# A graph layer with a mixer and experts: two bias rows added as one-row matmuls in PSUM instead of VectorE additions

## The reference, cut to what matters

```python
h = xn                                        # graph network, three layers
for l in range(3):                            # relu, relu, sigmoid
    agg = segment_sum(h[src], edge_type * N_NODES + dst)       # one sum for each relation and node
    h = act(einsum('rnd,rde->ne', agg.reshape(8, N_NODES, -1), W[l]) + h @ root[l] + bias[l])
...                                           # mixer
attn = qkv @ Wo + bo                          # bo: a row of 256
fx = attn + xn
h2 = layernorm(fx, ln2_g, ln2_b)
m = gelu(h2 @ W1 + b1) @ W2 + b2              # b2: a row of 256
mix = m + fx
```

## Time and profile before

| | |
|---|---|
| median of 3 runs | 6539.37 us (6536.87 to 6542.21) |
| the profiled execution's own time | 6533.36 us |
| its span, first to last instruction | 6531.2 us |
| PE busy | 5414.8 us (83%) |
| POOL busy | 4629.2 us (71%) |
| DVE busy | 2018.7 us (31%) |
| ACT busy | 1063.2 us (16%) |
| mean granted TensorE clock | 0.920 |

### The profile page before, as it was taken

One profiled execution on the slowest core, in us unless ns is written; L12 is line 12 of the kernel. 1 busy time (PEld: TensorE's weight loads), 2 busy tenths in 40 slices (PEclk: granted clock), 3 DMA queues, 4 the chain that ended last, 5 costly groups with the idle time before them and its releaser, 6 DMA issues.

```text
span 6531.2 us, 82572 instructions
## 1 busy us (share of the span) xinstructions
PE 5414.8 (83%) x22990; PEld 4056.3 (62%) x22990; DVE 2018.7 (31%) x5385; ACT 1063.2 (16%) x2755; POOL 4629.2 (71%) x4909
## 2 busy tenths in 40 slices
PE   8977777777777778888888888887888888888888
PEld 3445555555555546666666666665777777777776
DVE  3321211121221223232323333333444444444444
ACT  2211111111111111111111111111222222222222
POOL 1057777777777767777777777776777777777775
PEclk9988888888888889999999999999999999999999
DMA  6654444444444444555445444445333334333433
GB/s 194 180 154 137 137 137 136 137 137 137 137 137 137 137 143 145 147 145 146 146 148 149 147 145 147 146 146 149 115 115 115 116 115 115 115 116 115 115 115 90
DMA packets 354283, 887.87 MB, mean 136 GB/s; under 512 B 86138, under 2 KB 179198, under 8 KB 335527
## 3 DMA queue, kind: packets, MB, share of 16 engines
q0 software_dynamic: 232080, 633.91, 33.1%
q10 hardware_dynamic: 114472, 243.54, 12.8%
q1 hardware_dynamic: 7350, 5.61, 0.3%
HBM read 697.11 MB, written 185.60 MB: 135 GB/s over the span
## 4 chain that ended last, share of the span: by engine, by line
POOL 48%; PE 27%; issue 16%; DMA 4%; ACTq 3%; ACT 1%; POOLq 1%; DVE 0%; DVEq 0%; SPq 0%
POOL ring L497 48%; PE ps_out L1381 10%; PE ps_y L1347 7%; DMA ring<-table,gather_idx 3%; PE ps_tr L1548 2%; PE ps_b L1536 1%; PE ps_c L1347 1%; PE ps_b L1347 1%; PE ps_c L1536 1%; PE ps_y L1634 1%; ACTq L609 1%; ACTq L730 1%; ACT y_stage L513 1%; ACTq L689 1%; ACTq L690 0%
## 5 line engine op out<-in xcount | busy, mean ns | idle before, releaser
L497 POOL DMA_INDIRECT ring<-table,gather_idx x4836 | 4584.5, 948 | 1517.8 <-issue 1487.1
L1381 PE MATMUL ps_out<-ring,onehot 128*125 x8400 | 2250.9, 421 | 708.8 <-SPq L424 670.2
L1381 PEld LDWEIGHTS ps_out<-ring,onehot 128*125 128x125 f32 x8400 | 1704.4, 210 | 1134.6 <-issue 858.8
L1347 PE MATMUL ps_y<-W,hT 128*125 128x512 f32 (+1 forms) x2400 | 1016.2, 563 | 0.9 <-ACT hT L560 0.9
L819 DVE COPY y_stage<-ps_y 125x512 f32<-125x512 f32 x150 | 103.7, 691 | 2427.8 <-PE ps_y L1347 2404.1
L1381 PE MATMUL ps_out<-ring,onehot_more 128*125 x2448 | 657.3, 418 | 135.8 <-SPq L424 91.2
L1347 PEld LDWEIGHTS ps_y<-W,hT 128*125 128x125 f32 x2400 | 455.4, 192 | 399.2 <-issue 372.0
L978 DVE TENSOR_TENSOR onehot<-targets,ps_out 128x500 f32<-128x500 f32 x1050 | 646.0, 670 | 172.2 <-issue 117.1
L1381 PEld LDWEIGHTS ps_out<-ring,onehot_more 128*125 128x125 f32 x2448 | 474.5, 203 | 290.1 <-issue 221.3
L513 ACT COPY y_stage<-ps_y 125x512 f32<-125x512 f32 x350 | 204.9, 585 | 1638.2 <-PE ps_y L1347 1633.0
L978 DVE TENSOR_TENSOR onehot_more<-targets,ps_out 128x250 f32<-128x250 f32 x612 | 240.8, 414 | 592.5 <-PE ps_out L1381 474.3
(11 more groups left out here) (194 smaller groups left out, 3224.3 us busy)
## 6 DMA issues: line engine op xcount, KB each, us to landing
table<-y_stage ACTq DMA_DIRECT2D x147, 896.0 KB
ring<-table,gather_idx POOLq DMA_INDIRECT x4836, 3.3
table<-y_stage ACTq DMA_DIRECT2D x147, 104.0 KB
xn_in<-xn_scratch ACTq DMA_DIRECT2D x100, 125.0 KB
base<-y_stage ACTq DMA_DIRECT2D x100, 125.0 KB
base_in<-base ACTq DMA_DIRECT2D x100, 125.0 KB
x_in<-in_x_dram ACTq DMA_DIRECT2D x76, 125.0 KB
xn_scratch<-xn_in ACTq DMA_DIRECT2D x50, 125.0 KB
```

The source lines that it names most:

```text
L497: nc.gpsimd.indirect_dma_start(ring[0:n, c * D:(c + 1) * D], None, table[l], bass.IndirectOffsetOnAxis(ap=gather_idx[0:n, tile:tile + 1].b ...
L1347: last = nc.tensor.matmul(BANK[phase][b][0:WIN, 0:n], hT[parity][:, k, :], W[:, k, b * 2 * D:b * 2 * D + n], start=(k == 0), stop=(k == K ...
L1381: return nc.tensor.matmul(ps_out[w % 2][0:WIN, 0:D], lhsT, ring[:, bass.ds(slot + j * D, D)], start=first, stop=last)
```

## The change

The row `bo` is multiplied by a column of ones, a matmul with one partition of contraction, that opens the accumulation group of `attention`. The row `b2` does the same ahead of the eight matmuls of `down_projection`. The two DVE additions of those rows go, and DVE's addition of the attention takes the normalised nodes as they were loaded.

```diff
-        S_CHAIN, P2_CHAIN, P3_CHAIN, R_CHAIN = 3, 15, 13, 9
+        S_CHAIN, P2_CHAIN, P3_CHAIN, R_CHAIN = 3, 13, 13, 9
@@ attended (DVE)
-                chain(nc.vector.tensor_tensor(fx[:, :], xn_in[parity][:, :], mix_bc[:, 0, :], ALU.add), done)
                 dve.wait_ge(attn_done, w + 1)
-                chain(nc.vector.tensor_tensor(fx[:, :], ps_a[0:WIN, 0:D], fx[:, :], ALU.add), done)
+                chain(nc.vector.tensor_tensor(fx[:, :], ps_a[0:WIN, 0:D], xn_in[parity][:, :], ALU.add), done)
@@ attended (DVE), the end
                 chain(nc.vector.scalar_tensor_tensor(out=r0[parity][:, :], in0=fx[:, :], scalar=0.5,
                                                      in1=x_in[parity][:, :], op0=ALU.add, op1=ALU.add), done)
-                chain(nc.vector.tensor_tensor(r0[parity][:, :], r0[parity][:, :], mix_bc[:, 1, :], ALU.add), done)
@@ down_projection (PE)
                 if w:
                     pe.wait_ge(res_ready, w)
+                nc.tensor.matmul(ps_tr[0:WIN, D:2 * D], ones_row[0:1, :], mix_bc[0:1, 1, :], start=True, stop=False)
                 for j in range(FJ):
                     pe.wait_ge(gelu_done, w * FJ + (j + 1))
                     last = nc.tensor.matmul(ps_tr[0:WIN, D:2 * D], gT[:, j, :], W2[:, j, :],
-                                            start=(j == 0), stop=(j == FJ - 1))
+                                            start=False, stop=(j == FJ - 1))
@@ attention (PE)
                 pe.wait_ge(qT_ready, w + 1)
-                nc.tensor.matmul(ps_a[0:WIN, 0:D], qT[:, :], kvWo[:, :], start=True, stop=True).then_inc(attn_done, 1)
+                nc.tensor.matmul(ps_a[0:WIN, 0:D], ones_row[0:1, :], mix_bc[0:1, 0, :], start=True, stop=False)
+                nc.tensor.matmul(ps_a[0:WIN, 0:D], qT[:, :], kvWo[:, :], start=False, stop=True).then_inc(attn_done, 1)
```

## The result

The changed kernel takes 6560.34 us (median of 7, 6551.0 to 6569.36) against 6539.37 us: ratio 1.0031, 95% interval 1.0022 to 1.004. That is 21 us or 0.3% slower, inside the stated range and on the far side of the bound for "no change". It also scatters over 18 us, the kernel before over 5. The profiled execution took 6554.28 us, span 6552.3 us.

A forecast was written before the change was run, and what follows sets the result against it. Layer 1 was taken as bound by POOL's gathers and an almost equal loop of PE and ACT. 20.7 + 4.9 - 20.5 + 0.4 = +5.5 us on 6539.4 gave 6545 us, range 6534 to 6565.

The forecast's parts named there:

- two almost equal clocks: Layer 1: POOL's gathers, 40.3 us a window, and a loop of PE's work, then 9.7 us of ACT before xhatT.
- likeliest case: The forecast of +5.5 us, 6545 us, own range 6538 to 6552; given 46% for -1 to +13 us.
- `b2` in `down_projection`: Row's matmul between table product and down_projection, hidden by nothing: 0.43 us in each of 48 windows, 20.7 us.
- one partition streams slowly: Rival: one-row matmuls in both places take 1.0 us each, sum +45 us, 6585 us; chance 9%.
- `bo` in `attention`: Row's matmul mostly hidden while PE's sequencer reads the loop bound: 0.1 us in each of 49 windows, 4.9 us.
- both matmuls are paid in full: Rival: in the attention the sequencer's gap stays behind both matmuls, +21.7 us, 6561 us; chance 24% including mixtures.
- Room: PE's waits for data in layer 1 that the loop can use up before the layer's end moves: 20.5 us.
- issue gap: PE's idle behind attention, before more_units, while its sequencer reads the loop bound: 0.65 us, to become 0.2 to 0.3.
- Tail: Attention's one time on the chain, before layer 2: two matmuls of 0.43 come, one addition of 0.46 goes, +0.4 us.
- The clock: Rival: less idle around the attention keeps PE's clock up, 29 us come back, POOL sets the end, 6537 us; 18%.
- The port: DVE's additions lengthen POOL's gathers; some 3 us less for POOL, counting only if POOL sets layer 1's end.
- three signs of being wrong: Layer 2 starting over 15 us later, one-row records 0.4 us or more apart, half-clock stretches behind the attention changing in number.

The follow-up runs named there:

- b2_ident: Changed kernel with the b2 row brought in by a 125 by 125 identity and 125 copies of the row: 6530.45 us against 6531.53 before, ratio 0.9999.
- b2_rows32: Changed kernel with the b2 row brought in over 32 rows, the first of ones, the others zero: ratio 1.0043 to the kernel before, in a paused session.
- b2_gap: Changed kernel with the one-row b2 matmul moved behind the attention and bo on DVE: ratios 1.0016, then 0.9994 to the kernel before, both in paused sessions.
- bo_only: Changed kernel with the b2 row back on DVE, only bo by TensorE: 6526.54 us against 6531.53 before, ratio 0.9993.
- no_rows: Kernel with both rows left out of the computation, on DVE and on PE: 6523.79 us against 6531.53 before, ratio 0.9989.
- b2_only: Changed kernel with the bo row back on DVE, only b2 by TensorE: 6548.79 us against 6531.53 before, ratio 1.0026.
- after_loads_later_2: Second run of the changed kernel with ACT making xhatT ahead of its three loads: ratio 1.0 to the kernel before, in a paused session.

## Why the prediction was right in its range and wrong in its size

The mechanism was right: two almost equal clocks, the loop's room used up, and then PE sets the end. The sum was +5.5 us and the profiled executions differ by 20.9 us. That the time lies in the range is in part luck. It is outside the likeliest case's own range, 6538 to 6552, and the upper end that covers it was the full price of both rows: 21.1 us for `bo`, which cost nothing, stood in for what was missing at `b2`.

From the first attention of layer 1 to the last it was 1993.0 us before and is 2015.4 after, +22.4. Counted from start to start of PE's records this is 39.0 for `b2`, 1.0 for `bo`, -21.1 of waits for data in the written-out units, -2.7 of waits for `xhatT`, and 6.2 for the rest, mostly the clock. (By the first gathers of the two layers, above, it was 21.9.) Ahead of the layer 1.1 us were lost, and behind it some 2 us won. Term by term:

- **`b2` in `down_projection`: the step that failed.** It was charged 0.43 us by the stream of full-height matmuls and measures 0.82, 39.0 us instead of 20.7. Those 18.3 us are the size of the miss: with them alone the sum is +24. The prediction gave both ends, 0.43 and 1.0, and chose by the read pattern of line 1304; what mattered was the height of the weight tile. The price stood in the trace of before, in the 8-row matmul of line 1657, nearer in height than the attention's 32 rows and in the midst of a full-height stream, as `b2` is. The rival "one partition streams slowly" therefore had more for it than line 1304, though its 1.0 us is too high and its price for `bo` wrong. `b2_ident`, `b2_rows32` and `b2_gap` show the cause.
- **`bo` in `attention`:** charged 4.9 us, measured 1.0 over 49 windows, next to nothing (1.35 us before and 1.31 after in the windows shown; `bo_only` no slower). The reading that the sequencer goes on while the matmuls stream was right. The rival "both matmuls are paid in full" gave 6561 us, the measured time, by the wrong mechanism: its place was the attention. (Its sum passes 13 us from a charge of 0.25 us a window on, not 0.27.)
- **Room, 20.5 us:** PE's wait for data fell by 25 us, of which 4.3 were the issue gap. Right.
- **Tail, +0.4 us:** the stall grew by 0.7. Right in kind.
- **The clock,** which had a rival but no term. It gave nothing back, it took, some 6 us. On the page of after the first half of `up_projection` reads as below; before it was 153.7 us, mean 369.

```profile
L1534 PE MATMUL ps_b<-xhatT,big 128*128 128x125 f32 x800 | 168.4, 394 | 162.8 <-ACT xhatT L714 162.8
```

More of it ran at 1.2 GHz, behind PE's 3 to 4 us of idle for `xhatT`: +14.7 us. Other groups gave part of that back, the plain units 5.6 us and the second half of `up_projection` 1.6. Over the layer PE streamed at half clock for 284.2 us instead of 266.4, and the mean granted clock in 2480:4480 fell from 0.93 to 0.92. Why it reaches further is open. It is no mere effect of a longer loop: `no_rows` stood at 168.0 us in the first half of `up_projection` and at 290.2 us of half clock, and lost no time by it, since POOL set its pace; `b2_only` had 167.9 and `b2_ident` 158.7. The scatter of the changed kernel may have to do with it: over its seven timed runs the mean granted clock was 0.916 to 0.921, and the fastest run, 6551.0 us, had the highest, but the slowest, 6569.36, had 0.918.
- **The port:** 3 us were charged to POOL, `no_rows` shows some 6 in the gathers, of which 2 are directly the two rows', and 8 in all. In the changed kernel POOL no longer sets the layer's end, so by the prediction's own condition it does not count. The direction of the Trainium skill's rule ("SBUF — State Buffer", Who interferes with whom) holds here, at 4 ns a gather; the prediction's estimate of 42 us for a full block is seven times the 6 us.

Of the signs named ahead, the shrunk issue gap (0.19 us), the vanished wait for data, the shrunk wait in the last window (2.2 us at most, from 7.8), the unchanged wait for `xhatT` and the gathers nearer to 946 ns came as said. The one-row records lie 0.31 us apart, not 0.21. POOL's wait for PE grew not by little but from 9.1 to 39.8 us. Two of the three signs of being wrong came: layer 2 starts 23 us later, over the 15 named, and the half-clock stretches behind the attention changed in number. The eight records there take over 2.5 us in 23 windows instead of 18.

## What to carry to other kernels

Price a small matmul by what stands on both sides of it, not by its columns: in this stream of full-height fp32 matmuls a tile of 1, 8 or 32 rows lost the overlap of the weight loads on both sides, 0.38 us beyond its columns for one row, and the same sum over 125 rows lost none. Look in the trace for a small matmul that already stands in such a stream; its steps give the price. A matmul put where PE waits for its sequencer was free here, so look for such a place before taking an operation off an engine that has time. And where two engines' periods are within 1% of each other, count the slower loop's room in microseconds over the whole stage; it is the budget of any change, and the engine with the larger share of the chain does not show it.

## What the runs showed of the hardware

**Weight loads and the height of the tile.** From full height (128 rows) to 1, 8 or 32 rows and back, the records start about 0.31 us apart instead of 0.22, four times for a bias row, and the weight loads have 0.33 us without a load ahead of them. From 32 rows to 1 row (`b2_gap`), from 1 to 32 (0.216 us, the attention of the changed kernel) and from 128 to 125 and back (`b2_ident`) there is no break. The Trainium skill ("TensorE: Matmul & The Clock Gate", The mechanism, under the packing of small matmuls) says that weight loads are pulled ahead of matmuls in flight when their row group does not conflict or when they go to the background weight buffer, and, of its traces, that they overlap only when the row group differs. The last does not hold here: loads of full height run ahead of one another at 0.216 us a step, and those between full height and 1, 8 or 32 rows do not.

**The clock behind an idle.** PE's idle of 3 to 4 us for `xhatT` is followed by matmuls at half the full clock, in the changed kernel at a mean of 394 ns where they take 276 without the idle (`after_loads_later_2`). In this group that is 168.4 us against 98.2, but no run shows that the layer gets the 70 us back, since the half clock moved to other groups there.
